# Graph-attention layer on one core: eight 256 KB transfers per adjacency row tile, in the order of quarters 0, 2, 1, 3, in place of four of 512 KB

## What is computed

```python
def reference(x, adj, W, w1, b1, w2, b2):      # x 4096x128 f32, adj 4096x4096 int32
    in_fts = W @ x.T
    f1 = (w1 @ in_fts).T + b1
    f2 = (w2 @ in_fts).T + b2
    logits = f1 + f2.T
    bias_mat = where(adj > 0, 0.0, -1e9)
    coefs = softmax(leaky_relu(logits) + bias_mat, axis=-1)
    return layernorm(x + coefs @ x, axis=-1)
```

## Time and profile before

| | |
|---|---|
| runs | 392.08, 393.35, 393.64 us |
| median | 393.35 us |
| span of the profiled execution, first to last instruction | 391.8 us |
| its own time | not listed apart from the runs; the median is 1.55 us above this span |
| busy in the span | PE 287.4, DVE 285.5, ACT 241.0, POOL 105.7 us |
| moved | 73.69 MB, mean 188 GB/s |

### The profile page before, as it was taken

The page is one execution under the profiler, slowest core; times in us unless marked ns, Lnnn a source line. Parts: engine busy times, 40 slices in busy tenths (PEclk is TensorE's granted clock), DMA queues, the critical chain, the costliest instruction groups (busy, mean ns, idle before and its releaser), DMA issues.

```text
span 391.8 us, 5975 instructions
## 1 busy us (share of the span) xinstructions
PE 287.4 (73%) x2163; PEld 229.0 (58%) x2164; DVE 285.5 (73%) x415; ACT 241.0 (62%) x373; POOL 105.7 (27%) x83
## 2 busy tenths in 40 slices
PE   4779859691948876299819990999289936995492
PEld 3335538580846765288708880788168834884382
DVE  3769989827666575988397939693979388757994
ACT  2759986999293289625984498439861997010120
POOL 1744673005000040502050124004220414040641
PEclk9966968897996999599968997799869995999599
DMA  7999991999999999989999999999999999992001
GB/s 166 219 208 252 219 210 33 211 209 207 209 209 208 208 211 209 211 184 208 224 209 205 207 224 209 208 210 224 209 205 210 208 225 207 208 210 49 27 0 57
DMA packets 25762, 73.69 MB, mean 188 GB/s; under 512 B 3088, under 2 KB 7312, under 8 KB 25744
## 3 DMA queue, kind: packets, MB, share of 16 engines
q1 hardware_dynamic: 25168, 73.48, 91.1%
q10 hardware_dynamic: 576, 0.00, 0.1%
HBM read 71.37 MB, written 2.10 MB: 188 GB/s over the span
## 4 chain that ended last, share of the span: by engine, by line
DMA 60%; DVE 24%; issue 5%; SPq 5%; PE 2%; POOL 1%; DVEq 0%; POOLq 0%
DMA nat<-in_adj 59%; DVE mnt L593 11%; SPq L291 4%; DVE masks L608 3%; DVE post L585 2%; DVE masks L617 1%; POOL sgn L366 1%; DMA masks<-in_x 1%; DVE post L584 1%; SPq L285 1%; DVE mnt L599 1%; DVE ybt L771 1%; DVE rng L710 1%; PE ps L941 0%; PE ps L977 0%
## 5 line engine op out<-in xcount | busy, mean ns | idle before, releaser
L977 PE MATMUL ps<-bt,masks 128*128 128x258 f16 x2048 | 253.8, 289 | 85.1 <-DVE masks L608 85.0
L977 PEld LDWEIGHTS ps<-bt,masks 128*128 128x128 fp8e5 x2048 | 210.4, 103 | 128.3 <-issue 82.8
L447 ACT ACTIVATE sgn<-f1b,nf2l 128x512 int8<-128x512 f32 (+1 forms) x256 | 186.7, 852 | 2.2 <-DVE nf2l L646 1.6
L593 DVE TENSOR_SCALAR mnt<-nat 128x4096 fp8e5<-128x4096 int32 x32 | 76.2, 2384 | 83.2 <-DMA nat<-in_adj 83.1
L501 ACT ACTIVATE post<-ps,ac 128x258 f32<-128x258 f32 x64 | 26.5, 469 | 107.6 <-PE ps L977 107.6
L608 DVE SCALAR_TENSOR_TENSOR masks<-sgn,pat,mnt 128x256 uint32<-128x256 uint32 x128 | 67.8, 599 | 1.5 <-DVE mnt L599 1.4
L399 POOL TENSOR_TENSOR isox<-xsum,iso 128x516 f32<-128x516 f32 x7 | 17.9, 2557 | 140.5 <-DVE rec L761 140.5
L617 DVE SCALAR_TENSOR_TENSOR masks<-sgn,mnt 128x2048 uint32<-128x2048 uint32 (+2 forms) x18 | 42.2, 2346 | 0.0
L599 DVE STREAM_TRANSPOSE mnt<-mnt 128x1024 uint32<-128x1024 uint32 x32 | 37.9, 1220 | 0.0
L379 POOL TENSOR_TENSOR bt<-post,bt 128x1032 f16<-128x1032 f32 x8 | 22.3, 2782 | 18.8 <-ACT bt L462 18.8
L388 POOL TENSOR_TENSOR post<-post 128x1032 f32<-128x1032 f32 x7 | 17.8, 2539 | 24.7 <-ACT post L501 24.6
(11 more groups left out here) (85 smaller groups left out, 112.9 us busy)
## 6 DMA issues: line engine op xcount, KB each, us to landing
nat<-in_adj SPq DMA_DIRECT2D x128, 512.0 KB, 12.4
masks<-in_x SPq DMA_DIRECT2D x16, 128.0 KB, 4.6
out<-ybt SPq DMA_DIRECT2D x7, 256.0 KB, 16.0
out<-post SPq DMA_DIRECT2D x4, 64.0 KB, 2.3
wsb<-in_L_gnn_W SPq DMA_DIRECT2D x1, 64.0 KB, 2.3
w<-in_L_gnn_w ACTq DMA_DIRECT2D x2, 0.5 KB, 2.7
b<-in_L_gnn_b ACTq DMA_DIRECT2D x2, 0.5 KB, 3.6
xn<-in_x SPq DMA_DIRECT2D x1, 0.5 KB, 31.3
```

What stands on the lines that cost most here:

```text
L447: ins = act.activation(sgn_b[s][:, b, :, k], f1b[:, bass.ds(q * QW, QW)], ACT.Sign, bias=nf2l[:, n:n + 1], scale=-1.0)
L593: dve.tensor_scalar(mnt[:, 0, c * NK * P:(c + 1) * NK * P].bitcast(FP8), nat[:, c, :], 0, None, ALU.is_gt, saturate=False).then_inc(cast_d ...
L977: return pe.matmul(ps[:, 2 * c + m, 0:2 * DV], mask_f[slot][m][:, n // KB, n % KB, c * P:(c + 1) * P], btv[m][:, n, :], start=start, stop= ...
```

## The change

Each row tile comes as eight transfers. The four row groups are halved (groups 0 and 1, then groups 2 and 3), and for each half the four quarters are taken in the order 0, 2, 1, 3. A transfer is 32 partitions times 2 groups times 4 KB, 256 KB. The pieces of 4 KB are the same ones, to the same places. As a transfer adds 16 to the semaphore, the waits for a full slot count to twice as much.

```diff
             def load_adj(t, slot):
-                for a in range(A):
-                    dst = nat[a * SQ:(a + 1) * SQ, slot, :].rearrange("s (g c) -> s g c", g=G)
-                    sp.dma_start(dst, adj_v[t, a]).then_inc(nat_in[slot], 16)
+                for h in range(2):
+                    rows = slice(h * G // 2, (h + 1) * G // 2)
+                    for a in (0, 2, 1, 3):
+                        dst = nat[a * SQ:(a + 1) * SQ, slot, :].rearrange("s (g c) -> s g c", g=G)[:, rows]
+                        sp.dma_start(dst, adj_v[t, a][:, rows]).then_inc(nat_in[slot], 16)
...
-                    sp.wait_ge(nat_in[s], 2 * 16 * A)
+                    sp.wait_ge(nat_in[s], 2 * 16 * 2 * A)
...
-                dve.wait_ge(nat_in[c], 16 * A * (u + 1))
+                dve.wait_ge(nat_in[c], 16 * 2 * A * (u + 1))
```

## The result

Three runs of the changed kernel took 373.02, 373.48 (the median) and 374.55 us, against 393.35 before. The ratio is 0.9513, with a 95% interval of 0.9479 to 0.9546: 4.9% faster. The forecast was 373, in a range of 342 to 384. The profiled span is 372.6 us, against a forecast of 371.4.

What follows compares the result with a forecast made beforehand. The prediction took the DMA engines at 209 GB/s as the bound. Tiles 4 to 15 give 10.9 us and four quads 9.5, together 20.4: span 391.8 to 371.4, plus 1.55 makes 373 us, range 342 to 384.

Steps and rivals of the forecast that it cites:

- What bounds the kernel: Steady part: goes at the pace of the DMA engines, 209 GB/s, 10.03 us a tile.
- More passages: Tile loads: eight steps a tile between quarters 0, 1 and quarters 2, 3, not two; 234 GB/s, 1.07 us less a tile.
- More issues on SP: SP's queue: four more transfers a tile, 2.0 us more of SP's time, costing nothing; uncovered, up to 2.0 us a tile.
- The price of a transfer: DMA engines: any fixed price of a transfer is already in the 234 GB/s of `x`, so nothing is added.
- What is late next: Pairs with `moments`: DVE frees a slot late, queue dry from T + 17.3 to T + 19.2, a 1.9 us gap each.
- T: In DVE's work on a pair of tiles: the time when the pair's odd tile lands and its cast starts.
- The sum: Whole span: 10.9 us less in tiles 4 to 15, 9.5 in four quads, together 20.4; prelude and tail stay.
- Nothing gained: Steady part: the 234 GB/s of `x` does not come from passages, a tile keeps 10.03 us; 393 us, chance 0.09.
- a price for each transfer: DMA engines: starting each added transfer holds them up, 0.93 us a tile more, 26 us; 419 us, chance 0.09.
- The engines spread further: DMA engines: drift until half are in each pair of quarters, towards 294 GB/s, 7.13 us a tile; 340 us, chance 0.12.

Runs made afterwards that it cites:

- Size_only: The changed kernel with its eight 256 KB transfers a tile in quarter order 0, 0, 1, 1, 2, 2, 3, 3 (two passages): 392.54 us.
- order_only: The kernel before with its four 512 KB transfers a tile in quarter order 0, 2, 1, 3 (four passages): 385.10 us.
- halves_0123: The changed kernel with its eight 256 KB transfers a tile in quarter order 0, 1, 2, 3, twice (four passages): 384.43 us.
- dest_alternates: The changed kernel, columns read from HBM in order 0, 1, 2, 3 but written to partition ranges in order 0, 2, 1, 3: 370.92 us.
- source_alternates: The changed kernel, columns read from HBM in order 0, 2, 1, 3 but written to partition ranges in order 0, 1, 2, 3: 384.00 us.
- sixteen_grouped: Against the kernel before, sixteen 128 KB transfers a tile, the four of one quarter one behind the other (two passages): 396.83 us.
- the early cast: Kernel before, with DVE casting the next even tile ahead of the minus masks in odd pairs with `moments`: 383.23 us.
- early_cast_after: The changed kernel, with DVE casting the next even tile ahead of the minus masks in odd pairs with `moments`: 361.0 us.

## Why the prediction was right, step by step

**What bounds the kernel: right.** Wherever the rate of the full queue changed, the time changed with it, with no work of PE, DVE or ACT altered.

**More passages: right, in mechanism and size.** 234 GB/s and 8.96 us a tile were forecast from `x`, and 234 was measured. At 201 GB/s a tile takes 10.43 us; two passages give 10.03, four (215) 9.75, eight (234) 8.96: 0.20, 0.17 and 0.18 us for each. Size_only, order_only and halves_0123 show that it is the count of passages, and dest_alternates and source_alternates that they are passages between partitions. No run here is without any passage; the 201 is that of windows inside a tile.

**More issues on SP: right at 256 KB, and near its end.** Nothing was lost to them. At 128 KB SP is the bound.

**The price of a transfer: right to put at nothing.** It is 0.01 us at most.

**What is late next: the place was right, one step of it wrong.** The queue runs dry once a quad, behind `moments`. But the step "the queue had two tiles left at T - 0.6: before, enough until T + 19.5, so nothing was lost" failed. T is when the slowest engine finishes, and by then the others have moved a good part of the next tile. From T = 143.5 the changed kernel moved 232 GB/s x 15.3 us = 3.55 MB, and the queue was dry by 158.5, where two tiles are 4.19 MB: 0.64 MB, a third of a tile or 2.7 us at 234 GB/s, had gone ahead. The landing records of tile 11 show more than half of it directly: its last sixteen come from 141.27 to 143.39 us, on the mean 1.46 us ahead of the last. How the rest divides is not shown. It is less where the engines lie closer: from T = 182.26 to 200.50, when nothing moved any more, 210 GB/s x 18.24 us = 3.83 MB were moved, so 0.36 MB had gone ahead, with the last sixteen of tile 15 on the mean 1.02 us ahead of the last. Behind tile 11 the gap came at T + 15, not T + 17.3, and lasted about 3 us, not 1.9; new bytes flowed at T + 18.5, a little ahead of the T + 19.2 of the prediction. Over 13 us about each hole (from 153, 193, 232, 270 and 310 us) the rates are 171, 190, 198, 194 and 204 GB/s, so against 234 the five cost 3.5, 2.4, 2.0, 2.2 and 1.7 us, 11.8 in all for a forecast 9.5. The same step hid that the kernel before already ran short, by 1.8 us in all, although the 184 among its slices and the 131 GB/s from 169 to 171.5 us showed it. In the difference of the two kernels the two mistakes largely cancel: 10.0 us for a forecast 9.5. Of the 9.5 us that moving the cast gave the kernel before, this explains the smaller part.

**The sum.** Tiles 4 to 15 gave 192.15 - 182.26 = 9.9 us for a forecast 10.9, the four quads 162.95 - 154.16 = 8.8 for 9.5, and the tail 0.5 for nothing. The span fell by 19.2 for 20.4. The profiled execution was the slowest of the three (374.55 us), so the median stands 0.9 above its span, not 1.55, and less of the shortfall shows in the time than in the parts; that 373.48 lies within half a microsecond of 373 is partly luck.

**The rivals.** *Nothing gained* and *a price for each transfer* are excluded by the rate and by sixteen_grouped. With the first falls, for a queue kept full, the rule of the Trainium skill, SBUF — State Buffer, section "Can I just issue two DMAs to hit both halves?": transfers to the lower and the upper 64 partitions do overlap here, at each passage, and 259 GB/s with sixteen of them is 29% above the 201 without any. *The engines spread further* did not happen as described, though a milder form of it is real in the kernel before: with the early cast the rate there rises above what the count of passages gives, from 209 to 216 GB/s between the stores. The changed kernel shows little of it: early_cast_after reads 240 from 170 to 310 us with the stores' bytes counted, some 7 GB/s of it, and its 35.8 us a quad, a store included, are 4 x 8.96.

```profile
170.00:310.00 140.00, 118.22 (x987) 99.39 (x986) 115.41 (x155) 110.16 (x176) 40.04 (x32) 0.93 1.02 240
```

## What to carry to other kernels

Where each transfer fills 32 partitions, order the transfers so that each goes to the other half of the partitions than the one ahead of it, and make them as short as the issuing engine can keep up with (128 KB at 0.50 us an issue here). This is shown for one queue, kept full, on one core. When transfers get faster, work out anew when each buffer comes free: the engine that frees it, and not the transfers, may decide, and moving its cast ahead of other work was worth 12.5 us on top of the 20 of the change. Look for rates that differ between stretches of one trace before believing that a full DMA share is full speed: 209 and 234 GB/s both read 1.04 to 1.07.

## What the runs showed of the hardware that was not expected

- The DMA engines do not end a transfer together. The last sixteen landing records of a tile lie 0.4 to 2.3 us apart in the kernel before (tiles 5 to 31), and a queue can be short for some of them 2 us ahead of the landing (share 0.90 and 172 GB/s), so "two tiles in the queue" lasts less long than their bytes at the mean rate: some 15 us from T on in place of 17.3 in the changed kernel.
- What a passage gains is not fixed. With two passages a tile and the early cast, the rate between the stores went from 209 to 216 GB/s, and it was back at 211 when the 256 KB stores were taken out, although they are themselves traffic in the same queue. Why is not shown.
- SP issues one transfer of 128 KB in 0.50 us, 96 of them in 48.35 us, as long as it takes for one of 512 KB. At 128 KB this caps the rate at 260 GB/s.
